# Work moved from GpSimd and VectorE to ScalarE and VectorE in a Mamba and mixture-of-experts kernel

## The reference

```python
x_in = einsum('ed,bld->bel', in_proj_w, ctx)                  # 512 channels from 256
u = silu(causal_conv4(x_in) + conv_b)
x_dbl = einsum('ke,bel->bkl', x_proj_w, u)                    # 16 for dt, 16 for B, 16 for C
delta = softplus(dt_proj_w @ x_dbl[:, :16] + dt_proj_b)
A = -exp(A_log)                                               # 512 channels x 16 states
def step(state, (d_t, B_t, C_t, u_t)):                        # over 512 tokens
    state = state * exp(d_t[..., None] * A) + (d_t * u_t)[..., None] * B_t[:, None, :]
    y_t = einsum('ben,bn->be', state, C_t)
y = (y + D * u) * silu(z)                                     # z = layernorm(x), laid out as channels x 512
x = x + tanh(g_xattn) * y
out = x + tanh(g_ffn) * moe(layernorm(x))                     # 8 experts, the best 2, and a shared one
```

## Time and profile before

| | us |
|---|---|
| median of 3 runs | 658.73 |
| lowest and highest | 657.96, 660.96 |
| the profiled execution | 659.18 |
| its span, first to last instruction | 657.4 |

### The profile page before, as it was taken

The page is one execution under the profiler, slowest core; times in us unless marked ns, Lnnn a source line. Parts: engine busy times, 40 slices in busy tenths (PEclk is TensorE's granted clock), DMA queues, the critical chain, the costliest instruction groups (busy, mean ns, idle before and its releaser), DMA issues.

```text
span 657.4 us, 7506 instructions
## 1 busy us (share of the span) xinstructions
PE 507.8 (77%) x2304; PEld 254.5 (39%) x2304; DVE 507.1 (77%) x560; ACT 398.7 (61%) x757; POOL 494.3 (75%) x240
## 2 busy tenths in 40 slices
PE   5505535688897788954499799975997997989998
PEld 4202211246462355611143233331443443656766
DVE  4577898767999899986877999967879779873211
ACT  4549667788635776494478654454798855671340
POOL 4289999879998859897939989979677799950000
PEclk9657777869797897966599889966999799899989
DMA  2596723543265231346521323054310644001001
GB/s 81 166 388 200 244 64 129 195 176 114 80 210 174 80 117 35 99 165 240 164 90 59 128 86 108 24 193 156 125 61 22 225 160 134 11 1 59 22 17 48
DMA packets 39940, 79.70 MB, mean 121 GB/s; under 512 B 5977, under 2 KB 12761, under 8 KB 39900
## 3 DMA queue, kind: packets, MB, share of 16 engines
q1 hardware_dynamic: 39900, 79.23, 35.7%
HBM read 62.17 MB, written 17.04 MB: 120 GB/s over the span
## 4 chain that ended last, share of the span: by engine, by line
PE 30%; DVE 28%; issue 15%; ACT 13%; POOL 10%; DMA 3%; ACTq 0%; POOLq 0%; DVEq 0%; SPq 0%
DVE decay L1220 10%; PE wk L1528 7%; PE wk L1514 7%; POOL ring L979 7%; DVE ring L1220 6%; PE y_ps L1449 4%; ACT decay L1055 3%; PE wk L1465 3%; DVE ring L1234 3%; DVE u L1246 2%; ACT L1024 2%; DMA dd<-dd_scratch 2%; ACT z L1090 2%; POOL ring L1001 2%; PE wk L1490 1%
## 5 line engine op out<-in xcount | busy, mean ns | idle before, releaser
L979 POOL TENSOR_TENSOR ring<-dd,b_in 128x2048 f32<-128x2048 f32 x64 | 289.2, 4531 | 12.2 <-issue 8.9
L1055 ACT ACTIVATE decay<-dd,a_neg 128x255 f32<-128x255 f32 (+1 forms) x384 | 188.1, 533 | 40.6 <-DVE ring L1220 40.4
L1001 POOL TENSOR_TENSOR ring<-ring,c_in 128x2048 f32<-128x2048 f32 x32 | 144.8, 4525 | 21.9 <-DVE ring L1220 20.7
L1220 DVE TENSOR_TENSOR_SCAN ring<-decay,ring 128x1024 f32<-128x1024 f32 x64 | 144.6, 2278 | 13.6 <-ACT decay L1055 7.0
L1220 DVE TENSOR_TENSOR_SCAN decay<-decay,ring 128x1024 f32<-128x1024 f32 x64 | 146.2, 2285 | 11.2 <-ACT decay L1055 7.8
L1514 PE MATMUL wk<-xc,w_down 128*128 128x256 f32 (+1 forms) x432 | 133.3, 463 | 6.4 <-DVE xc L1302 3.8
L1528 PE MATMUL wk<-h,w_up 128*128 128x256 f32 (+1 forms) x432 | 136.0, 471 | 0.5 <-DVE h L1395 0.5
L1449 PE MATMUL y_ps<-ring,fold 128*32 128x256 f32 (+1 forms) x768 | 79.4, 560 | 60.7 <-DVE ring L1234 60.4
L1514 PEld LDWEIGHTS wk<-xc,w_down 128*128 128x128 f32 x432 | 81.1, 193 | 55.6 <-issue 44.5
L1528 PEld LDWEIGHTS wk<-h,w_up 128*128 128x128 f32 x432 | 83.5, 198 | 44.3 <-issue 35.2
L1234 DVE TENSOR_TENSOR ring<-decay,c_in 128x1024 f32<-128x1024 f32 x64 | 78.4, 1225 | 7.0 <-DVE decay L1220 0.5
(11 more groups left out here) (105 smaller groups left out, 444.3 us busy)
## 6 DMA issues: line engine op xcount, KB each, us to landing
dd<-dd_scratch SPq DMA_DIRECT2D x64, 256.0 KB, 3.1
dd<-dd_scratch SPq DMA_DIRECT2D x32, 512.0 KB, 4.2
b_in<-bc_scratch SPq DMA_DIRECT2D x8, 512.0 KB, 5.6
c_in<-bc_scratch SPq DMA_DIRECT2D x8, 512.0 KB, 4.4
dd_scratch<-dd_out SPq DMA_DIRECT2D x16, 256.0 KB, 3.2
z<-in_x SPq DMA_DIRECT2D x4, 1024.0 KB, 7.3
x<-in_xT SPq DMA_DIRECT2D x4, 1024.0 KB, 6.6
dd_scratch<-dd_out SPq DMA_DIRECT2D x8, 512.0 KB, 4.2
```

The costliest lines, as they stand in the source:

```text
L979: nc.gpsimd.tensor_tensor(two, dd[:, j % DD_RING:j % DD_RING + 2, None, n:2 * n].broadcast_to([P, 2, TILES[v], n]), b_in[:, None, g % BC_R ...
L1001: nc.gpsimd.tensor_tensor(two, two, c_in[:, None, g % BC_RING].broadcast_to([P, 2, WIDE]), ALU.mult).then_inc(weighed_pool, 2)
L1055: last = nc.scalar.activation(decay[:, i % 2, q * n + 1:(q + 1) * n], dd[:, j % DD_RING, 1:n], ACT.Exp, scale=a_neg[:, c, r, k:k + 1])
L1220: last = nc.vector.tensor_tensor_scan(to, decay[:, i % 2], ring[:, i % RING], 0.0, ALU.mult, ALU.add)
```

## The change

Four things change. First, `DVE_GROUPS = (0, 1, 2, 31)`: in these four groups VectorE forms the products of all four slots, not of two, and their scans write to `decay`. Second, the products of VectorE are no longer part of a slot's turn behind its scan, but steps of `PLAN` with times of their own (`weigh_d`). Third, the copies of last states of VectorE's slots go to ScalarE (`keep`), which makes them before the buffer is reset. Fourth, z's statistics are made by ScalarE: for each row block a Copy of 512 columns in place with a sum, for all a Copy that turns sums into minus means, then two Squares of 256 columns each with the sum of squares; GpSimd's `affine_z` adds the halves. `ident` loses its own tile and lies in `xc`. All lists of `PLAN` are new.

```diff
-    return i % NR4 in POOL_WEIGHS
+    return i % NR4 in POOL_WEIGHS and i // NR4 not in DVE_GROUPS
...
+def keeps(i):
+
+    return sum(goes_on(PLACES[j][0]) and not weighs_on_pool(j) for j in range(before_slot(i) // NR4 * NR4 + NR4))
...
     "gate": [
-        [4.5, 9.5, 14.5, 17.5],
-        [21.5, 25.333, 29.5, 35.667],
-        [40.75, 50.1, 58.667, 64.5],
-        [74.5, 84.5, 91.667, 96.143],
-        [101.333, 106.5, 109.111, 112.667],
-        [121.5, 123.5, 125.667, 128.133],
+        [5.75, 10.25, 13.5, 17.5],
+        [22.667, 25.5, 30.5, 34.333],
+        [42.667, 50.5, 58.333, 66.667],
+        [74.667, 82.5, 91.333, 98.5],
+        [102.667, 110.5, 111.333, 112.727],
+        [122.333, 123.5, 125.333, 128.129],
     ],
...
     "stats_z": [
-        [2.2, 2.4, 2.6, 2.8],
+        [2.25, 2.5, 2.75, 3.5],
         [],
-        [37.333, 37.5, 37.667, 37.833],
-        [67.167, 67.5, 67.667, 67.833],
-        [97.167, 97.333, 97.667, 97.833],
+        [36.571, 36.714, 37.333, 37.667],
+        [70.25, 70.5, 72.25, 72.5],
+        [101.091, 101.273, 101.455, 101.727],
         [],
     ],
...
+    "weigh_d": [
+        [2.333, 2.667, 3.5, 5.25, 5.5, 7.25, 7.5, 9.333, 9.667, 10.5, 12.333, 12.667, 16.333, 16.667],
+        [20.333, 20.667, 23.5, 24.333, 28.333, 28.667, 32.333, 32.667],
+        [35.333, 36.333, 40.25, 40.5, 43.5, 45.25, 48.25, 48.5, 51.667, 53.333, 56.333, 56.667, 60.167, 60.333,
+         64.25, 64.5],
+        [68.25, 68.5, 71.667, 72.667, 75.333, 76.5, 80.333, 80.667, 84.333, 84.667, 88.333, 88.667, 91.667, 92.5,
+         95.5, 97.333],
+        [100.25, 100.5, 104.333, 104.667, 108.333, 108.667, 111.667, 112.364],
+        [116.25, 116.5, 120.5, 120.75, 123.75, 124.5, 125.667, 127.333, 127.667, 128.032],
+    ],
...
+            def keep(i):
+
+                v, c, p, r = PLACES[i]
+                if goes_on(v) and not weighs_on_pool(i):
+                    k, n = p * TILES[v], COLS[v]
+                    nc.scalar.activation(carry[:, c * NR4 + r, k:k + TILES[v], None],
+                                         decay[:, i % 2].rearrange("p (q n) -> p q n", n=n)[:, :, n - 1:n], ACT.Copy).then_inc(kept, 1)
...
                         act.wait_ge(weighed_dve, weighs(i - 1, False))
+                    keep(i - 2)
                 reset(i)
+                if i > 1 and kept_of(i - 2):
+                    act.wait_ge(kept, kept_of(i - 2))
...
+            def stats_z(b, k):
+
+                pair = range(2 * (k % 2), 2 * (k % 2) + 2)
+                if k == 0:
+                    act.wait_ge(z_loaded, DMA * (b + 1))
+                    if b > 0:
+                        act.wait_ge(z_scale, 4 * b)
+                if k < 2:
+                    for c in pair:
+                        nc.scalar.activation(z[:, c, :], z[:, c, :], ACT.Copy, accum_out=z_sum[:, c:c + 1]).then_inc(z_stats, 1)
+                if k == 1:
+                    act.wait_ge(z_stats, Z_STEPS * b + NW)
+                    nc.scalar.activation(z_ln[:, 1], z_sum[:], ACT.Copy, scale=-1.0 / L).then_inc(z_stats, 1)
+                if k > 1:
+                    for c in pair:
+                        for half in range(2):
+                            act.wait_ge(z_stats, Z_STEPS * b + NW + 1 + 2 * c + half)
+                            nc.scalar.activation(z_scrap[:], z[:, c, half * L // 2:(half + 1) * L // 2], ACT.Square, bias=z_ln[:, 1, c:c + 1],
+                                                 accum_out=z_var[:, c, half:half + 1]).then_inc(z_stats, 1)
...
             def scan(i):
-                v, c, p, r = PLACES[i]
-                n, j = COLS[v], c * NR4 + r
                 dve.wait_ge(outer_ready, i + 1)
                 dve.wait_ge(exp_ready, i + 1)
                 to = ring[:, i % RING] if weighs_on_pool(i) else decay[:, i % 2]
                 last = nc.vector.tensor_tensor_scan(to, decay[:, i % 2], ring[:, i % RING], 0.0, ALU.mult, ALU.add)
-                if goes_on(v) and not weighs_on_pool(i):
-                    steps[0] += 1
-                    last.then_inc(scan_step, 1)
-                    dve.wait_ge(scan_step, steps[0])
-                    k = p * TILES[v]
-                    last = nc.vector.tensor_copy(carry[:, j, k:k + TILES[v], None],
-                                                 to.rearrange("p (q n) -> p q n", n=n)[:, :, n - 1:n])
                 last.then_inc(scanned, 1)
...
             for slot in range(START[NU]):
                 what_is_due(slot)
                 scan(slot)
-                if not weighs_on_pool(slot):
-                    weigh(slot)
             what_is_due(START[NU])
```

566 lines of the change are left out of this document (285 added, 281 removed), and 64 rows, old and new, of the table PLAN.

## The result

The changed kernel takes 664.93 us (median of 6 runs, 661.65 to 665.41) against 658.70 for the kernel before (6 runs, 657.96 to 660.96). The ratio is 1.0081, with a 95% interval of 1.0055 to 1.0106: it is slower, by 5.3 us by this ratio and by 6.2 by the medians, where I had forecast 7.6 faster. The profiled execution has a span of 663.5 us and a time of 665.21.

What follows compares the result with a forecast made beforehand. VectorE and GpSimd were taken to alternate as last in the loop, with TensorE setting the tail. Terms -4 (units 0 and 1), -10, +3 and +3.4 gave -7.6 us, so 651.1 us against 658.70; range 638 to 669.

Steps and rivals of the forecast that it cites:

- The start: Stretch up to the first scan, 36.2 us: the change was said to hardly touch it, so nothing was counted.
- the -10 of units 2 to 5: Units 2 to 5: VectorE loses 11.8 us of statistics and copies, counted at its busy share of 0.85.
- Unit 0: First unit of the loop: forecast to grow from 64.9 to 72 us, +7 at unit 1's first scan.
- six exposed pairs: Unit 0: six products behind the next scan delay exponentials, each costing 1.0 us.
- 4 for gates that wait longer: Unit 0: 4 us added for gates that wait longer.
- (d): Products apart from scans: outside unit 0 and group 31, bounds of -4 and +12 us, taken as 0.
- Unit 1: Second unit: -11 us, near the ceiling of 13.6 us taken off GpSimd, which was last there.
- Group 31: Last stretch: two more products on VectorE and one exposed pair, 2.45 + 0.95 = +3.4 us.
- rival B: Units 3 to 5 and tail: TensorE gives back what the loop gains; no change, 658 us; chance 0.18.
- the +3 for ScalarE's bursts: Units 2 to 5: statistics bursts on ScalarE stick out, 3 batches at 1.0 us.
- (e): New written order of all engines, gates, routing and mixing later: counted as nothing, bound -7.5 us.
- A: Rival, slower: unit 0's +7 us is carried to the end, pairs cost 6.4 us more; 668.5 us; chance 0.22.

Runs made afterwards that it cites:

- e1: The changed kernel with the biases' splitting on VectorE put back behind unit 1's first convolution; 661.41 us, ratio 1.0020.
- e17: e7 with the start's order from the kernel before: unit 1's fourth in_proj behind three of four dt products, its read behind theirs; 661.49 us, ratio 1.0001.
- e7: e4 with z's statistics made by VectorE again; 655.29 us, ratio 0.9918.
- e6: e4 with every product of VectorE right behind its scan again; 657.59 us, ratio 0.9965.
- e14: e13 with each product of VectorE in unit 0 right behind its scan; 660.24 us, ratio 1.0004.
- e15: e7 with every product of VectorE right behind its scan; 656.21 us, ratio 0.9921.
- e4: e1 with group 31's first two products given back to GpSimd; 657.86 us, ratio 0.9965.
- e8: The kernel before, with only all products of groups 0 to 2 moved to VectorE, each right behind its scan; 668.60 us, ratio 1.0133.
- e5: e4 with the first two products of groups 0 to 2 also back on GpSimd; 657.68 us, ratio 0.9957.
- e11: e4 with statistics on VectorE, no group wholly VectorE's and products right behind scans; last-state copies stay on ScalarE; 664.36 us, ratio 1.0052.
- e13: e7 with groups 0 to 2 back on GpSimd, products still apart from scans; 659.64 us, ratio 0.9993.
- e3: e1 with TensorE's sums of group 25 after three of nine down products, gate, residuals and a GpSimd product placed to match; 665.62 us, ratio 1.0075.

## Why the prediction was wrong, point by point

The forecast was -7.6 us in the span, the measurement +6.1. Of the 13.7 us between them 6.2 are at the start, 5.6 in units 2 to 5, and 1.9 in units 0 and 1.

**The start (forecast 0, measured +6.2).** This is the step that failed most, and most of what made the kernel slower; the other is the -10 of units 2 to 5, below. I said that the change hardly touches the start, because I had looked for added and removed work there. But in the lists the biases and a convolution changed places, and what counted was the order on VectorE's queue, the bank of wk between it and TensorE, and a chain of 21 us behind it without slack. e1 shows 5.0 us of it. For the other 1.2 there is the fourth in_proj of unit 1 in front of the dt products: e17, which moves it back, has its first scan at 36.0 us, 2.6 before e7's and 1.4 before e1's.

**Unit 0 (forecast +7, measured +7.8).** The number held by luck, as its parts didn't. I had six exposed pairs at 1.0 us; e6, e14 and e15 measure 1.0 to 2.7 for all of them. I had 2 us for ScalarE's part of the statistics; e7 has 1.7 less in unit 0, but its first scan of unit 1 is only 0.5 earlier than e4's. I had 4 for gates that wait longer, and what there is instead is 4.5 from the lists alone, a wait for exponentials behind table loads. The groups by themselves cost 7.4 in the old lists (e8) but 1.4 in the new ones (e4 against e5), and nothing by the first scan of unit 1 (110.0 and 110.3 us). In the new lists VectorE has idle time for them: its scans wait 6.7 to 9.9 us for exponentials in unit 0 of e4 and e5, and 0.3 in the kernel before. Parts that hide one another don't add. The trace has the six late products that I counted in unit 0, but 21 more, not 18: three stand behind the first scan of the next group, and by my price they add 3 x 0.45 us to (d)'s bound.

**Unit 1 (forecast -11, measured -9.9).** The number held for the wrong reason, which is luck too. I took it from the relief of GpSimd. e8 gives GpSimd this relief and unit 1 gains nothing; e5 takes it away on the new lists and unit 1 stays short (65.9). It comes from the lists: e11 has 8.8 of it with no move but that of the last states' copies, as VectorE has 53.2 us of work in this unit now and 62.2 before, and feed-forward steps are put off. The relief is worth at most the 3 to 4 us of e7 against e13 and of e15 against e14. Put-off work is not a gain, and my step should have asked where the work goes.

**Units 2 to 5 without group 31 (forecast -10 + 3 = -7).** Group 31 taken at 3.4 us, the stretch from unit 2 to the end has -3.4 + 0 + 7.0 - 1.6 = +2.0 in all, so -1.4 without it. Two terms failed. The -10 was VectorE's ledger times its busy share. A busy share of 0.85 doesn't say that VectorE is last: units 3 and 4 kept their 218.2 us while VectorE had 7.6 us less to do in them (121.3 + 63.2 before, 109.4 + 67.5 now), and its scans waited 19.2 us there for exponentials instead of 7.1. What holds these units is open. TensorE's work is as much as before (119.2 + 67.7, 105.1 + 83.1), as rival B would have it, but GpSimd's is as well, and the chain that ended last has more of ScalarE and less of TensorE than before (see 3). And the +3 for ScalarE's bursts had a batch at 6.3 us where it is 7.5. I took the sum's read as nothing; it is an instruction of its own, within the bound of 2.2 us a batch that I had given. What the move cost in the changed kernel is small: e7 against e4 has 2.6 us (ratios 0.9918 and 0.9965, whose intervals just don't touch), and at like clocks hardly that.

**Group 31 (forecast +3.4).** e4 measures 3.55 us by the medians and 3.0 by the spans. The number held, in part by luck: 1.4 us of the 3.0 lie ahead of the end of the last product, where I had put all of it, and 1.7 behind it, at a higher clock that e3 has with the group on VectorE.

**(e), the gates.** Their wait fell by 11.8 us, beyond the -7.5 that I gave as the bound, and the time didn't follow: scans wait 27.7 us longer for exponentials. A wait that is the largest in its table is not yet the limit.

**The rivals.** A had the sign, but its mechanism, a delay of unit 0 carried through unit 1, didn't happen. No rival had an edit at the start, nor the lists as a cause. The rule of the Trainium skill that I had cited ("ScalarE: Activation LUTs", Rules for kernel authors: adds and multiplies belong on VectorE) agrees with the engine times, 3.4 us a batch against 7.5, but not always with the whole: statistics on VectorE are 29 us ahead with the old lists and 1.4 to 2.6 with the new ones and groups on VectorE, but 2.0 to 6.5 behind with the new ones and no groups there. Where they differ, the runs decide.

**What would show it.** GpSimd 476 us (475.8), VectorE about 500 (496.8), ScalarE about 430 (429.9) came out. The first scans of units 1 and 2 were to be near 108 and 173 us; they are at 115.1 and 181.5, of which 6.2 are the start. The stretch behind the last product was 67.0, not longer.

## What to carry to other kernels

Read a diff of an order as carefully as a diff of work: two neighbouring steps of VectorE that changed places, one of them 4.4 us long, cost 4 to 5 us of the whole, through a bank that two unrelated results share. At a start without slack, follow every engine's queue up to the first step of the loop.

When a schedule is rewritten, a stage that gets shorter may only have handed its work on; compare sums over stages, and each part of a change on both orders, because a part that costs 29 us in one order costs 3 in the other, and gains 6 there when another part that gives the same relief is left out.

Before a difference of a few tenths of a per cent is put down to an edit, look at the granted clock of the executions behind it, and at more than four of them.

## What the runs showed of the hardware

A sum output of ScalarE is a second instruction, ACTIVATION_READ_ACCUMULATOR, 0.187 us long, 48 of them here. Its start lies 0.1 us before the end of the ACTIVATE, and behind a Copy the next instruction starts 0.1 us after it: from start to start it is 0.61 us for 512 columns, where a step of 512 columns without a sum between two of them took 0.48 (447.85 to 448.33 in the changed kernel), and 0.62 for 256 with a bias from memory and a wait.

One and the same program ran at mean granted clocks from 0.835 to 0.866, in two clusters 8 us apart and one execution between them (e17), while the kernel before stayed between 0.842 and 0.847 in the 23 executions beside it. The profiles of e7 and e17, one execution of each, differ in unit 1 (granted clock 0.84 and 0.73) and in unit 3 (0.93 and 0.88). They are two programs, so which stretches differ between executions of one isn't shown; e17's three fast executions were not the profiled one. The Trainium skill ("TensorE: Matmul & The Clock Gate", What's actually happening) says of the matmuls that run at the lower clock when a kernel starts that their number varies between runs of one kernel, and that their cost is below 1% of a typical span. Here it is the mean clock of a whole execution that varies, and the 9.3 us between the ends of e17 are 1.4%.
